# Queries and keys turned by DMAs that transpose, in place of TensorE, ScalarE and VectorE, in a two-layer attention and expert kernel

## The reference, cut to what matters

```
x = layernorm(x + attention0(x))     # q, k, v = x W + b; rotary embedding of q and k; 16 heads of 8
x = layernorm(x + experts0(x))       # 8 experts, each takes the 256 best tokens
x = layernorm(x + attention1(x))     # q = x W; k, v from a latent of 32; 16 heads of 8
x = layernorm(x + experts1(x))       # 16 experts, each token takes its 4 best
attention: softmax(q k^T / sqrt(8)) v per head over the 256 tokens of a batch, then an output product
```

## Time and profile before

| | |
|---|---|
| runs | 602.04 us median (600.29, 602.04, 603.62) |
| profiled execution | 603.38 us, span 601.6 us |
| busy | PE 90%, DVE 71%, ACT 69%, POOL 57% |
| mean granted TensorE clock | 0.939 |
| attention of layer 0 | about 15 to 126 us; of layer 1, about 252 to 367 us |

### The profile page before, as it was taken

How to read it: one execution, slowest core, us unless ns; L and a number is a source line. 1 busy time by engine, 2 the same in 40 slices (tenths; PEclk the granted TensorE clock), 3 DMA queues, 4 the chain that set the end, 5 groups by cost and what they waited for, 6 DMA issues and landing times.

```text
span 601.6 us, 16720 instructions
## 1 busy us (share of the span) xinstructions
PE 538.7 (90%) x5262; PEld 388.6 (65%) x5262; DVE 429.6 (71%) x1582; ACT 413.9 (69%) x1104; POOL 344.2 (57%) x471
## 2 busy tenths in 40 slices
PE   9899999999779984799999999979999999999950
PEld 7444444447557973544555444758889999999940
DVE  4979999966765304877989996786887788643276
ACT  2279998882624752538999988417778888999824
POOL 4978888342005782673445544456566777777730
PEclk9979999998999997958999999779999999999975
DMA  7493000002001237007910000112221122111363
GB/s 215 112 322 101 2 1 3 2 2 71 7 1 43 47 40 223 6 1 218 302 46 2 3 2 1 54 39 58 51 52 54 59 62 61 59 58 55 125 186 120
DMA packets 53204, 43.12 MB, mean 72 GB/s; under 512 B 14992, under 2 KB 43424, under 8 KB 52992
## 3 DMA queue, kind: packets, MB, share of 16 engines
q1 hardware_dynamic: 45568, 29.98, 17.3%
q0 software_dynamic: 7264, 11.62, 7.4%
q10 hardware_dynamic: 288, 0.46, 0.2%
HBM read 30.17 MB, written 11.87 MB: 70 GB/s over the span
## 4 chain that ended last, share of the span: by engine, by line
PE 70%; DVE 12%; issue 6%; DMA 5%; ACT 4%; POOL 2%; DVEq 0%; ACTq 0%; POOLq 0%; SPq 0%
PE bank L1329 12%; PE bank L1339 11%; PE bank L928 10%; PE bank L911 7%; PE bank L893 6%; PE bank L945 3%; ACT prob L1477 2%; DMA parts<-augs,idx_s 2%; PE bank L969 2%; DVE W L1965 2%; PE bank L1141 2%; PE bank L1382 1%; PE bank L1161 1%; PE bank L953 1%; PE bank L1200 1%
## 5 line engine op out<-in xcount | busy, mean ns | idle before, releaser
L1792 DVE TENSOR_REDUCE mx<-bank 128x2 f32<-128x512 f32 x256 | 163.1, 686 | 24.7 <-PE bank L893 23.7
L1477 ACT ACTIVATE prob<-bank 128x512 f32<-128x512 f32 x256 | 140.7, 609 | 23.0 <-PE bank L911 19.1
L1666 ACT ACTIVATE queries<-bank,prob 128x128 f32<-128x128 f32 x316 | 90.4, 369 | 19.9 <-PE bank L1329 17.0
L1329 PE MATMUL bank<-keys,prob 128*128 x632 | 85.7, 278 | 0.8 <-issue 0.6
L1339 PE MATMUL bank<-W,queries 128*128 x632 | 84.2, 276 | 0.0
L804 POOL DMA_INDIRECT prob<-xs,idx_g x64 | 61.8, 966 | 33.7 <-DVE idx_g L2176 12.6
L1329 PEld LDWEIGHTS bank<-keys,prob 128*128 128x128 f32 x632 | 76.8, 192 | 3.9 <-issue 2.6
L893 PE MATMUL bank<-keys,queries 32*128 32x256 f16 x512 | 77.0, 285 | 2.6 <-issue 1.7
L1339 PEld LDWEIGHTS bank<-W,queries 128*128 128x128 f32 x632 | 76.7, 192 | 1.8 <-issue 0.7
L928 PE MATMUL bank<-prob,augs 128*32 128x256 f32 x1024 | 77.7, 392 | 0.0
L813 POOL DMA_INDIRECT parts<-augs,idx_s x64 | 63.4, 991 | 21.5 <-issue 9.0
(11 more groups left out here) (292 smaller groups left out, 1045.3 us busy)
## 6 DMA issues: line engine op xcount, KB each, us to landing
W<-in_w SPq DMA_DIRECT2D x48, 256.0 KB, 4.0
sum<-zero SPq DMA_DIRECT2D x3, 1024.0 KB, 9.1
xs<-X SPq DMA_DIRECT2D x2, 768.0 KB, 5.2
prob<-xs,idx_g POOLq DMA_INDIRECT x80, 2.6
XB<-sum SPq DMA_DIRECT2D x1, 1024.0 KB, 4.9
Y<-sum SPq DMA_DIRECT2D x4, 256.0 KB, 5.7
W<-sum SPq DMA_DIRECT2D x4, 256.0 KB, 6.5
parts<-augs,idx_s POOLq DMA_INDIRECT x64, 2.2
```

The source lines that it names most:

```text
L1329: last = nc.tensor.matmul(bank[2 + p % 2][:, P * f:P * f + P], wc[:, p % 4, P * f:P * f + P], xsT2[:, bass.ds(at, 1), :], start=True, stop ...
L1477: nc.scalar.activation(prob[:, v % 8, :, :], st_bank(b, v)[:, :], ACT.Exp, scale=SCALE).then_inc(exp_done, 1)
L1666: last = nc.scalar.activation(hid2[:, p % 4, f, :], bank[2 + p % 2][:, P * f:P * f + P], ACT.Gelu, bias=wc[:, p % 4, WB + f:WB + f + 1])
L1792: nc.vector.tensor_reduce(m_at, bank[S1B[u % 2]][:, :].rearrange("p (j k) -> p j k", j=2), AX.X, ALU.max).then_inc(s1_used, 1)
```

## The change

For batches 1 to 7 of each layer the turning goes to SyncE: once a tile's split is ready, one transposing DMA (256 KB) moves all 32 heads of it from `aug` to `qkT`, now three buffers holding queries and keys together. `aug_ready` counts tiles rather than batches, so the first tile's DMA can start before the second tile is done. A batch's DMAs wait that those of the batch before have landed, and that the batch three before is no longer read. Batch 0 is still turned by TensorE. GpSimd splits batch i+1 ahead of copying the values of batch i. SyncE's order is rewritten: the first turn stands ahead of the constants, and the experts' weights come in portions between the turns.

```
-        QT = [queries[...] for i in range(2)]
-        keyT = [keys[...] for i in range(2)]
+        qkT = [keys[:, 1024 * i:1024 * i + 1024].bitcast(F16).rearrange("p (t c l) -> p t c l", t=2, l=P) for i in range(3)]
...
                 engine.tensor_tensor(A[:, t, 0:H, 2 * HD:3 * HD], s4[:, t, 0:H, :], A[:, t, 0:H, 0:HD],
                                         ALU.subtract)
-                last = engine.tensor_tensor(A[:, t, H:2 * H, HD:2 * HD], s4[:, t, H:2 * H, :],
-                                               A[:, t, H:2 * H, 0:HD], ALU.subtract)
-            last.then_inc(aug_ready, 1)
+                engine.tensor_tensor(A[:, t, H:2 * H, HD:2 * HD], s4[:, t, H:2 * H, :],
+                                     A[:, t, H:2 * H, 0:HD], ALU.subtract).then_inc(aug_ready, 1)
...
+            def turn(lay, b):
+
+                g = b + NB * lay
+                if b > 2:
+                    sp.wait_ge(st_done, 16 * (g - 2))
+                wait_for(sp, turned_in, 32 * (g - 1 - lay))
+                for t in range(2):
+                    sp.wait_ge(aug_ready, 2 * g + t + 1)
+                    sp.dma_start_transpose(qkT[b % 3][:, t, :, :], aug[b % 2][:, t, :, :].rearrange("p h x -> p (h x)")
+                                           ).then_inc(turned_in, 16)
+
+            def batches_in(lay):
+
+                at = ((0, 0, 4, 8, 8, 8, 8, 8), (0, 0, 3, 6, 9, 12, 15, 16))[lay]
+                for b in range(1, NB):
+                    turn(lay, b)
+                    if lay == 0 and b == 1:
+                        constants_in()
+                    if lay == 1 and b == 2:
+                        sp.wait_ge(join_xt, 4)
+                    for e in range(at[b - 1], at[b]):
+                        expert_weights(lay, e)
+                    if lay == 0 and b == 4:
+                        sums_zeroed()
...
             def pool_iteration(lay, i, par):
 
-                build_vaug(lay, i, par)
                 if i < NB - 1:
                     build_aug(pool, lay, i + 1, 1 - par)
+                build_vaug(lay, i, par)
...
+                if i > 0 and u == 0:
+                    pe.wait_ge(turned_in, 32 * (g - lay))
...
                     if u == 13 and tail_on:
                         out_transposes(lay, i - 2)
-                    if u == 13 and front_on:
-                        query_transposes(lay, i + 1, nxt)
                     if u == 15 and tail_on:
                         out_product(lay, i - 2)
-                    if u == 15 and front_on:
-                        key_transposes(lay, i + 1, nxt)
...
-                elif i > 0:
-                    keys_evac(lay, i, par, 1)
...
-                if front_on:
-                    keys_evac(lay, i + 1, nxt, 0)
...
-                    if u == 13 and front_on:
-                        q_evac(lay, i + 1, nxt)
```

More of the change, by code:

```diff
@@ L599, in expert_weights, with constants_in @@
                 sp.dma_start(W[:, at, W2AT:WROW].rearrange("p a (t c) -> p (a t) c", c=P), src3).then_inc(w_in, 16)
[L602 to L607, removed]
+            def constants_in():
+                for n, dst in (("tri", tri), ("steps_at", steps_at), ("half_col", half_col), ("from_less", from_less), ("triX", triX), ("triC", triC),
+                               ("same_col", same_col), ("before", before), ("ends", ends), ("dexp", dexp), ("slot_in", slot_in),
+                               ("tile_at", tile_at), ("slot_at", slot_at), ("expert_at", expert_at), ("nibble", nibble),
+                               ("row_base", row_base)):
+                    sp.dma_start(dst[:], d["c_" + n]).then_inc(consts_in, 16)
+            def turn(lay, b):
[19 more added lines that the diff above has]
+                        sums_zeroed()
             tiles = lambda ap: ap.rearrange("(t p) c -> p t c", p=P)
@@ L660, in choices_in, with sums_zeroed @@
                                  runs(d["parts"][TOK * (TOPK - 1):TOK * TOPK, :])[:, at, :]).then_inc(end_back[c], 16)
[L662 to L666, removed]
+            def sums_zeroed():
+                sp.wait_ge(zeroed, 2)
+                for n in range(3):
+                    sp.dma_start(runs(sums_d[n]), zero[:, 0:P].unsqueeze(1).to_broadcast([P, NT, P])).then_inc(scratch_in, 16)
+            batches_in(0)
             tokens_out(0)
             sums_in()
-            experts_in(1)
+            batches_in(1)
             tokens_out(1)
@@ L892, in s1 @@
                 for j in range(2):
[L893 to L894 removed]
+                    last = nc.tensor.matmul(bank[S1B[u % 2]][:, L * j:L * j + L], qkT[i % 3][rows, qt, 2 * jp + j, :],
+                                            qkT[i % 3][rows, :, NJ + 2 * jp + j, :], start=True, stop=True)
                 last.then_inc(s1_done, 1)
@@ L1109, in m5_read @@
             def m5_read(b, g):
[L1111 to L1114, removed]
+                if b > 2:
+                    pe.wait_ge(tq2_ready, 2 * (g - 2))
             def front_latent(lay, b, par):
@@ L1155, in query_transposes @@
                 g = b + NB * lay
-                pe.wait_ge(aug_ready, g + 1)
-                if not (isinstance(b, int) and b in (0, NB - 1)):
-                    pe.wait_ge(qkv_ready, 2 * g + 4)
+                pe.wait_ge(aug_ready, 2 * g + 2)
                 for j in range(NJ):
                     for t in range(2):
-                        last = nc.tensor.transpose(half[M5][:, L * j + P * t:L * j + P * t + P],
+                        last = nc.tensor.transpose(half[M5][:, P * (4 * t + j):P * (4 * t + j) + P],
                                                    aug[par][:, t, 4 * j:4 * j + 4, :], ident_h[:, :])
@@ L1166, in key_transposes @@
                 g = b + NB * lay
-                pe.wait_ge(aug_ready, g + 1)
-                if not (isinstance(b, int) and b == 0):
-                    pe.wait_ge(kt_ready, 2 * g)
+                pe.wait_ge(aug_ready, 2 * g + 2)
                 for j in range(NJ):
                     for t in range(2):
-                        last = nc.tensor.transpose(half[M6][:, L * j + P * t:L * j + P * t + P],
+                        last = nc.tensor.transpose(half[M6][:, P * (4 * t + j):P * (4 * t + j) + P],
                                                    aug[par][:, t, H + 4 * j:H + 4 * j + 4, :], ident_h[:, :])
@@ L1566, in keys_evac @@
                 g = b + NB * lay
[L1567 to L1571, removed]
+                act.wait_ge(tk_done, lay + 1)
+                at = slice(NJ + 2 * pair, NJ + 2 * pair + 2)
+                turned = half[M6].rearrange("p (t j l) -> p t j l", t=2, l=P)
+                nc.scalar.copy(qkT[b % 3][:, :, at, :], turned[:, :, 2 * pair:2 * pair + 2, :]).then_inc(kt_ready, 1)
             def front_evac(lay, b, par, t):
@@ L1851, in q_evac @@
             def q_evac(lay, b, par):
[L1852 to L1856, removed]
+                dve.wait_ge(tq_done, lay + 1)
+                nc.vector.tensor_copy(qkT[b % 3][:, :, 0:NJ, :], half[M5].rearrange("p (t j l) -> p t j l", t=2, l=P)
+                                      ).then_inc(tq_ready, 1)
             def norm(lay, b, pair):
```

26 lines of the change are left out of this document (11 added, 15 removed).

## The result

The changed kernel takes 630.4 us, the median of four runs (627.7 to 632.5); the kernel before took 602.8 beside it. The ratio is 1.045 (95% interval 1.037 to 1.052), so it is 27.6 us slower. The forecast was slower by 12, with 632 as the end of the range: direction and place of the loss were right, its size was less than half.

A forecast was written before the change was run, and what follows sets the result against it. VectorE, ScalarE and GpSimd were taken as near their limit, handing work round in a ring. Terms 8.0 + 4.8 + 1.0 - 0.6 - 1.2 = +12 us on 602 gave 614 us, own range 608 to 619, 8 in 10 600 to 632.

The forecast's parts named there:

- +3.03 - 0.43 - 0.61 = +2.0 us, period 16.2: Layer 0, iterations 2 to 5: ScalarE's copy 3.03 us later, 0.43 absorbed on TensorE, 0.61 saved on VectorE.
- the clock rival: Idle time lowers the granted clock, or ScalarE's exponentials lag: 1 us more in eight iterations, 622 us; chance 0.10.
- slow DMAs: Rival: both transposing DMAs land only 10 us after the second split, 640 us; chance 0.19, half of it beyond 632.
- The stall at full clock: Iterations 2 to 5, late value copy holding ScalarE's front_evac: +8.0 us in layer 0, +4.8 in layer 1.
- the start of the copy: ScalarE's front_evac in projecting iterations begins about 7.75 us after m_ready in layer 0, 7.1 in layer 1.
- Iteration 1 of layer 0: Values end at 35.05 or 34.4, copy stood at 32.62 already: +0.5 us after the saving.
- cover of 4.6: Batch 1: split ends at 22.3, s1 began at 26.86, leaving 4.6 us for the transposing DMAs.
- 4.0 after the second tile: Transposing DMAs take 4.0 us after the second tile and are hidden everywhere, 0 us.
- each two-byte element: Transposing DMAs: one packet per element would be 8192 x 37 ns = 300 us per DMA; left out, 1024 runs assumed.
- The saving: VectorE's copy of the queries goes: 0.61 us per batch.
- iteration 7: Last iteration of each layer: 0 us.
- Between the stages: The change touches nothing outside the two attention stages; iteration 0 of layer 1 cancels to 0.

The follow-up runs named there:

- g3: Changed kernel with 16 idle matmuls on TensorE ahead of the second projection of each iteration with maxima, a repeat on another chip: ratio 1.0265.
- e2: Kernel before with only GpSimd's order changed, split ahead of values, no transposing DMA: ratio 1.044.
- e3: Changed kernel in its own order (split first) with a third buffer for vraw: ratio 0.986.
- g2: Changed kernel with the third buffer for vraw, run again on another chip: ratio 0.989, 595.9 us against 603.1.
- g1: Changed kernel run again, unmodified, against the kernel before on the same chip: ratio 1.0445, 630.9 us against 603.1.
- e5: Kernel before with split ahead of values and a third buffer for vraw, no transposing DMA: ratio 0.9995.
- e6: Changed kernel with third vraw buffer, plus 14 idle matmuls ahead of batch 1's first score product in each layer: ratio 0.991.
- e7: Changed kernel with third vraw buffer and each transposing DMA issued twice, the second into unused space: ratio 1.013.
- g4: Changed kernel with third vraw buffer, plus 14 idle matmuls ahead of batch 1's first score product in layer 1 only: ratio 0.989.
- the first four experiments: Changed kernel with values first, 1.000; kernel before with split first, 1.044; changed kernel with three vraw buffers, 0.986; changed kernel with idle matmuls in the stall, 1.022.
- e0: Kernel before, unchanged, profiled on a chip where it takes 671 to 675 us.
- e1: Changed kernel with GpSimd copying the values ahead of the split again, transposing DMAs kept: ratio 1.000.

## Why the prediction was wrong in size, point by point

Differences in us against the first trace of the kernel before:

| stretch | forecast | changed | with idle matmuls (g3) |
|---|---|---|---|
| layer 0, to the end of iteration 0 | -0.6 | +0.6 | -0.4 |
| layer 0, iteration 1 | +0.5 | +2.2 | +2.1 |
| layer 0, iterations 2 to 5 | +8.0 | +12.0 | +7.4 |
| layer 0, iterations 6 and 7 | -0.6 | -0.3 | -0.3 |
| between, with iteration 0 of layer 1 | 0 | +3.6 | +2.2 |
| layer 1, iteration 1 | +0.5 | -0.3 | +0.6 |
| layer 1, iterations 2 to 5 | +4.8 | +8.4 | +5.1 |
| layer 1, iterations 6 and 7 | -0.6 | -0.3 | -0.3 |
| the rest | 0 | -1.7 | -0.3 |
| sum | +12 | +24.3 | +16.1 |

- **The step that failed** is the price of the stall, "+3.03 - 0.43 - 0.61 = +2.0 us, period 16.2" in layer 0 and +1.2 in layer 1, worked out from durations at clock 1.00. The prediction had the right mechanism, "the iteration's idle time lets the granted clock fall", as a rival with a chance of 0.10. The rival had it at 8 us (1 us in eight iterations); the runs put it at 11 us on one chip and 8 in the first trace. It should have been a term. The trace of before carried a warning. Of iterations 1 to 7 of each layer only iteration 1 is below the full clock (0.78 and 0.75), and it is the longest. In layer 0 TensorE stands idle four times just before the clock falls, for 0.20 to 0.72 us, the first time in the earlier trace rows, and its next projection takes 1.65 us in place of 0.91. The window and that projection:

```profile
27.40:42.90 15.50, 14.32 (x136) 5.74 (x136) 11.31 (x21) 11.21 (x24) 11.76 (x20) 0.78 1.05 310
```

```profile
30.86 1.65 PE L1141 MATMUL bank<-wqkv,XT 128*128 128x384 f32 x2
```

- **The range held by luck.** 630.4 us lies inside 600 to 632, but the upper end was there for slow DMAs, which did not come; the clock rival alone ended at 622.
- **The stall at full clock** was right: forecast +12.8 in the eight iterations, measured 7.4 + 5.1 = 12.5 (g3). So were its cause (e2, e3), its place and, within 0.3 us, the start of the copy.
- **Iteration 1 of layer 0** was sized too small, by 1.6 us. ScalarE's copy started at 35.96, 8.0 us after `m_ready`, as in the iterations behind it (7.9); the prediction had compared absolute times (34.4 to 35.05 against 32.62) and counted on an earlier `m_ready`, which came 0.6 later. The first DMAs were late there (2.14 us of wait), against the prediction's cover of 4.6: `s1` began 5.4 us after the second tile's split, where the prediction took 4.0; two issues of 1.30 us follow each other, and single landings take up to 4.7. But that is at most some 0.5 us of it: with a DMA wait of 1.6 to 1.9 us and no value stall, g2 took 15.23 and e3 15.98, the kernel before 15.50 and 15.30.
- **The DMAs hidden elsewhere: right** for the changed kernel, "4.0 after the second tile" against about 3.4 (2.8 from an issue that starts some 0.6 us after the split). The slow-DMA rival is out. So is the packet count of "each two-byte element": the queue shows 1056 packets for each of these DMAs, near the prediction's 1024. The Trainium skill (VectorE: DVE Perf Modes, The three transpose paths) gives 1309 ns for one 128x128 transpose by DMA. One DMA here turns eight such blocks and lands in 2.8 us, so the figure is not to be multiplied.
- **The saving** of 0.61 per batch was 0.52 in layer 0 and 0.63 in layer 1 where nothing stalls (g2). In iteration 7 the forecast of 0 was 0.2 too good.
- **Between the stages** 0 was forecast. Of the 3.6 us, about 0.9 lie in iteration 0 of layer 1 (0.88 in the first trace, 0.85 in g1). In g1, from the stage's first `front_evac` to `m_ready` it took 284.27 - 262.56 = 21.71 us, before 267.45 - 246.59 = 20.86, with a stall of 3.3 us on the value copy. The rest is not settled: on the slower chips the distance was 144.6 to 147.2 us for kernels of both kinds (146.8 before, 144.6 for e5, 147.2 for e6, 145.7 for e7), so 2 us of it may be scatter. On the chips where the kernel before takes 603 us the changed kernel showed 145.0 and 145.2, g2 to g4 142.3 to 143.5, and the only trace of the kernel before 141.4; whether the change itself costs something there is open.

> The kernel before, unchanged, profiled on the chip of these runs: attention iterations of 14.23 us in layer 0 and 14.36 in layer 1 as in the first trace, since the first four experiments showed attention iterations of the same length on a chip whose whole program takes 671 us. Between the two attention stages 141 us if that distance is a matter of the kernel, 147 us if it is one of the chip.

e0 gave those 146.8 us, and iterations of 14.24 and 14.36.

## What to carry to other kernels

When a change makes TensorE stand idle in a loop, price the stall twice: once by the timeline at the clock of now, and once with the work behind it at the clock's lower level, with durations from slow rows of the same trace (here 1.65 us for a projection in place of 0.91). Here the clock turned 16 us into 27. When one piece of work is moved ahead of another on a busy engine, look for a buffer whose release was the other's only duty: a third buffer of 1 KB a partition took the whole loss away and left the gain. A transposing DMA in place of TensorE's turn is worth what the saved PSUM copies were worth on the engine that bounds, if the data is ready early enough: about 6 us ahead of its reader was enough (g2: last split 7.1 us after `m_ready`, reader 13.1), and with the first DMA 1.3 to 4.4 us later some batches waited (e1).

## What the runs showed of the hardware

- A 256 KB transposing DMA from SBUF to SBUF: 1.23 to 1.31 us of issue on SyncE (single ones up to 2.8), landing mostly 2.7 to 2.8 us from issue, 5.7 at most (e1); a plain one of constants took 0.43 us to issue. The 28 of them added 29,568 packets, 1056 each.
- TensorE idle 2.36 us (changed kernel, iteration 5): the two matmuls of the next 128x384 projection took 1.51 us against 0.91, and 3.6 us after work resumed the value products took 0.64 us again.
- 16 idle matmuls in that gap (g3) held the clock at 1.00 and cost nothing measurable on the path: 16.10 us against 16.08 where the changed kernel kept 0.97, and 15.63 against 15.66 at 1.00 in layer 1.
